# Weighted sums of an MoE layer: each set of gathers waits until the preceding pair's gathers of that set have landed

## What is computed

```python
shared_out = (silu(x @ Wsg.T) * (x @ Wsu.T)) @ Wsd.T      # 704 hidden columns
topk_scores, topk_idx = top_k(softmax(x @ Wr.T), 2)       # 8 experts, 2 for each token
out_e      = (silu(x @ Wg[e].T) * (x @ Wu[e].T)) @ Wd[e].T
routed_out = w1 * out_e[first expert] + w2 * out_e[second expert]
x = x + gb * (routed_out + shared_out)
```

## Time and profile before

| | before |
|---|---|
| median of 3 runs | 1712.21 us |
| the profiled execution, its own time | 1702.0 us |
| its span in the trace | 1700.3 us |
| PE busy in the span | 1643.6 us (97%) |
| late units with the weighted sums | 1540 to 1652 us of the span |
| late units behind them | 1652 to 1696 us |
| POOL's 64 gathers, first and last start | 1540.1, 1637.5 us |

### The profile page before, as it was taken

How to read it: one execution, slowest core, us unless ns; L and a number is a source line. 1 busy time by engine, 2 the same in 40 slices (tenths; PEclk the granted TensorE clock), 3 DMA queues, 4 the chain that set the end, 5 groups by cost and what they waited for, 6 DMA issues and landing times.

```text
span 1700.3 us, 26873 instructions
## 1 busy us (share of the span) xinstructions
PE 1643.6 (97%) x8817; PEld 1426.7 (84%) x8817; DVE 1326.2 (78%) x2553; ACT 770.3 (45%) x1138; POOL 417.9 (25%) x505
## 2 busy tenths in 40 slices
PE   4899999999989999999999999999999999999998
PEld 1578788888768888888888888999999999998997
DVE  3999999998698788888788775777777777776872
ACT  2444434333445555454545423555555555552331
POOL 2254444343322111323232351000000000006740
PEclk9999999999999999999999999999999999999999
DMA  9622222322544443655554689788878888866861
GB/s 317 222 76 93 80 99 74 99 74 75 202 149 154 151 149 123 223 183 201 180 197 173 223 318 312 240 287 298 286 259 279 284 299 285 266 219 215 277 209 38
DMA packets 138980, 335.32 MB, mean 197 GB/s; under 512 B 20568, under 2 KB 20568, under 8 KB 133232
## 3 DMA queue, kind: packets, MB, share of 16 engines
q1 hardware_dynamic: 103904, 248.09, 43.6%
q10 hardware_dynamic: 24720, 52.21, 8.6%
q0 software_dynamic: 10240, 33.56, 5.7%
HBM read 230.21 MB, written 103.60 MB: 196 GB/s over the span
## 4 chain that ended last, share of the span: by engine, by line
PE 73%; DVE 15%; DMA 4%; issue 3%; SPq 2%; ACT 2%; POOL 1%; DVEq 0%; ACTq 0%; POOLq 0%
PE bank L701 17%; PE bank L703 17%; PE bank L702 17%; PE bank L712 5%; PE bank L2412 5%; PE bank L2410 5%; PE bank L2411 5%; PE bank L2405 2%; DVE stage L1714 2%; DVE mix L1793 1%; DVE xm_lo L1799 1%; DMA expert_in_rows<-y_rows 1%; SPq L798 1%; DMA mod_rows<-ca_rows 1%; PE bank L2394 1%
## 5 line engine op out<-in xcount | busy, mean ns | idle before, releaser
L701 PE MATMUL bank<-gu_hi,ex_x_hl 128*128 128x352 f32 x1080 | 359.9, 333 | 0.1
L703 PE MATMUL bank<-gu_hi,ex_x_hl 128*128 128x352 f32 x1080 | 348.5, 323 | 0.0
L702 PE MATMUL bank<-gu_lo,ex_x_hl 128*128 128x352 f32 x1080 | 348.4, 323 | 0.0
L1281 POOL DMA_INDIRECT raw<-expert_out_rows,out_slots x64 | 74.9, 1170 | 536.7 <-DMA expert_out_rows<-y_rows 513.0
L701 PEld LDWEIGHTS bank<-gu_hi,ex_x_hl 128*128 128x128 f32 x1080 | 203.7, 189 | 0.4 <-issue 0.3
L702 PEld LDWEIGHTS bank<-gu_lo,ex_x_hl 128*128 128x128 f32 x1080 | 204.0, 189 | 0.0
L703 PEld LDWEIGHTS bank<-gu_hi,ex_x_hl 128*128 128x128 f32 x1080 | 203.3, 188 | 0.0
L1888 DVE TENSOR_TENSOR hid<-bank,sg_t 128x352 f32<-128x352 f32 x135 | 70.2, 520 | 126.8 <-PE bank L703 107.7
L2410 PE MATMUL bank<-dn_hi,hid_hi 128*128 128x512 f32 x405 | 161.7, 399 | 3.9 <-DVE hid_lo L1892 3.9
L2412 PE MATMUL bank<-dn_hi,hid_lo 128*128 128x512 f32 x405 | 160.0, 395 | 0.0
L2411 PE MATMUL bank<-dn_lo,hid_hi 128*128 128x512 f32 x405 | 158.7, 392 | 0.0
(11 more groups left out here) (257 smaller groups left out, 3835.9 us busy)
## 6 DMA issues: line engine op xcount, KB each, us to landing
raw<-in_ex_gu SPq DMA_DIRECT2D x40, 1408.0 KB, 6.5
raw<-in_ex_dn SPq DMA_DIRECT2D x40, 512.0 KB, 4.7
ex_x<-expert_in_rows SPq DMA_DIRECT2D x71, 256.0 KB, 6.3
expert_out_rows<-y_rows ACTq DMA_DIRECT2D x71, 256.0 KB, 6.1
h_rows<-h_t SPq DMA_DIRECT2D x64, 256.0 KB, 2.6
h_turned<-h_hl ACTq DMA_DIRECT2D x32, 512.0 KB, 3.0
ex_x_hl<-h_turned ACTq DMA_DIRECT2D x32, 512.0 KB, 3.7
x_t<-in_x SPq DMA_DIRECT2D x32, 256.0 KB, 2.7
```

The costliest lines, as they stand in the source:

```text
L701: pe.matmul(acc, act_hi[i], w_hi[i], start=(i == 0), stop=False)
L702: pe.matmul(acc, act_hi[i], w_lo[i], start=False, stop=False)
L703: last = pe.matmul(acc, act_lo[i], w_hi[i], start=False, stop=(i == chunks - 1))
L1281: pool.indirect_dma_start(rows[:, pair % 2, a, :], None, ys_d, bass.IndirectOffsetOnAxis(ap=out_slots[:, k, n:n + 1], axis=0)).then_inc(ar ...
```

## The change

Two lines are added on POOL. From pair 1 on, ahead of the two gathers of a set, POOL also waits until both gathers of the same set of the preceding pair have landed (32 more on that slot's semaphore). It is done set by set: y1 of a pair waits for y1 of the pair before, y2 for y2. Nothing else is edited; lines behind it move down by two, so the gathers' line L1281 becomes L1283.

```diff
                     if pair >= 2:
                         pool.wait_ge(*(cb_vec.done(pair - 2, "both") if k else cb_act.done(pair - 2, "first")))
+                    if pair:
+                        pool.wait_ge((y2_in if k else y1_in)[(pair - 1) % 2], 32 * ((pair - 1) // 2) + 32)
                     for a in range(2):
                         n = 2 * pair + a
```

## The result

The changed kernel took 1725.41 us (median of 10 runs) against 1717.02 us for the kernel before in the same comparison (10 runs). The ratio is 1.0048, with a 95% interval of 1.0034 to 1.0061: about 8 us slower. One of the ten executions after the change took 2040.21 us and is left out of the ratio; the median holds with or without it to 0.5 us. The range of the prediction ended at 1721.5 us. In its own terms, as a difference, +8.2 us stands against a forecast of +3.2 us, and lies between it and the rival in which the chain becomes the bound (+11.3 us).

A forecast was written before the change was run, and what follows sets the result against it. PE, busy 97% of the span, was taken as the bound; +2.5 us for the chain of waits and +0.7 us for the ramp on the 1712.2 us median gave 1715.4 us, range 1709.5 to 1721.5 us.

The forecast's parts named there:

- the chain becomes the bound: Rival for the gather stage: long landings stay in every second pair and PE waits; +11.3 us, 1723.5 us, chance 0.12.
- Bound and path: PE, busy 97%, bounds; loss comes through late gathers, `weighted` on DVE, then `hid_of`; at most 4.3 us to gain.
- Cost of a met wait: On POOL, a new wait that has already been met costs nothing visible.
- The link: POOL's y1 gathers: step, 4.9 us landing and 0.3 us; 13.37 us per two pairs, 0.89 us too long.
- The expectation that gathers held back leave the burst: Last stage: gathers held back 2 us miss the store and load burst, so the 6.7 us landing isn't carried over.
- The sum behind the link: Pairs 4 to 15: six cycles of 0.89 us, 5.3 us, less 2.8 us of slack, +2.5 us.
- Slack: Gathers land ahead of use: y1 by 2.8 us before ACT, y2 by 2.1 us before `weighted`; delay within it is free.
- The ramp: Pairs 1 to 3: only pair 3's y2 gathers start later, costing 0 to 1.5 us; +0.7 us taken.
- The signs I named: Profile after: landings at most about 4.9 us, more `weighted` waits in even pairs, PE idle about 7.5 us, unchanged before 1540 us.
- Nothing happens: Rival: held-back gathers land in 4.3 us or less, or waits are nearly always met; 1712.2 us, chance 0.20.
- The 2.6 us to land: Gather landing by the skill page's rule: link 4.2 us against 6.24 us, no gather late, no cost; 1712.2 us.
- The queue is relieved: Rival: at most four gathers under way land sooner, PE's idle times go; -2.4 us at most, 1709.8 us, chance 0.18.

The follow-up runs named there:

- e1: The changed kernel with each wait moved to the landing of the pair two before, so always met; 1.0007 of the kernel before.
- e2: The changed kernel with the new waits kept for the y1 sets alone; 1.0055 of the kernel before.
- e9: The changed kernel, waits kept, with three slots for each set instead of two; 1.0057 of the kernel before.
- e8: The changed kernel with the new waits kept for pairs 1 to 3 only; 0.9993 of the kernel before.
- e4: The changed kernel with each set waiting for the set issued just before it, at most two gathers under way; 1.0501 of the kernel before.
- e14: The kernel before, no new waits, two slots, each pair's products made two late units later; 0.9957 of the kernel before.
- e15: The kernel before, no new waits, two slots, products two late units later, run again on one chip with three variants; 0.9970 of the kernel before.
- e3: The changed kernel with the new waits kept for the y2 sets alone; 1.0035 of the kernel before.

## Why the prediction was wrong

*Bound and path.* Right. PE bounds the stage, the loss came through `weighted` on DVE, the rest of the program was not touched, and no gain came.

*Cost of a met wait.* Right: e1, 1.0007.

*The link.* Here is the step that failed, in two of its three terms. The first is "A set may now start only 0.3 us (the issue step) behind the landing". I read 0.3 us between two gathers that POOL issues in a row and used it for a gather that had to wait; e2 shows 0.70 to 0.84 us. The second is the time to landing: 4.9 us was the median of all gathers, where the second of each set counts, which took 5.35 us on average in the links of e2. My links were (13.37 / 2 =) 6.69 us per pair, those of e2 7.45 us: 0.45 us more from the step behind the landing, 0.45 us more from the landing, 0.14 us less from the step between the gathers. The change thus made gathers lag 2.4 us per two pairs in e2 and 1.9 us in the profile after (14.4 against 12.48 us), where I had 0.89 us. The expectation that gathers held back leave the burst was half right: in e2 the median fell from 4.9 to 4.2 us, the worst stayed (7.9 us).

*The sum behind the link.* With the corrected step alone, the working gives (1.25 + 4.9 + 0.75) + (1.72 + 4.9 + 0.75) = 14.27 us for two pairs and 6 x 1.79 - 2.8 = 7.9 us. That this meets the measured 8.2 us is luck: it leaves the second gather's landing at 4.9 us and the clock at nothing. With all of e2's link it gives 6 x (14.89 - 12.48) - 2.8 = 11.7 us, where PE's idle time in e2 is 9.5 us above that of e1. Multiplying by six cycles therefore overstates somewhat; by which of its parts, no run shows.

*Slack.* I took off 2.8 us, the slack of y1, and treated y2's chain apart. In e2 the loss arrives through y2, held back behind y1 on POOL, so y2's 2.1 us was the slack to take. e9 shows besides that slack can't be had from slots alone.

*The ramp.* Mis-sized: 0.7 us put, nothing measured (e8).

*The clock* was missing from the sum. In the profile after it accounts for about 3 of the 12.2 us.

*The signs I named.* The median landing at or under 4.9 us (in e2; the profile after has none) and the more frequent waits of `weighted` came true, though the longest fell in odd pairs (5 and 9), not in even ones. POOL waited more often than said (13 times), PE's idle time rose to 13.5 us instead of 7.5 us, and a difference did arise before 1540 us, with the chip.

*Rivals.* "Nothing happens" is refuted by the loss itself. The 2.6 us to land that I estimated from the Trainium skill (DMA: Bandwidth & Descriptors, section "Anatomy of one DMA — SWDGE (gpsimd) path") do not agree with the traces: the gathers of before, e2 and e4 took 3.3 to 7.9 us. "The queue is relieved" saw a real effect, shorter median landings, which is worth less than the waits cost. "The chain becomes the bound" is what happened, at its threshold rather than at its full price; I gave it 0.12. The range ended 4 us short of the measurement, and that part is not the mechanism: it was set around a median of three runs, 1712.2 us, where ten runs gave 1717.0 us. As a difference it went up to +9.3 us, and +8.2 us lies inside.

## What to carry to other kernels

A wait that lets a transfer start only when the one before it has landed turns a queue into a chain of round trips. Work out the link with the landing of the last transfer of a set, under the load of that stage, and with the step from a landing to the next start of an engine that had been waiting; compare it with the consumer's pace, and ask what a small error costs over all the links. Look also at what stands behind the waiting instruction on its engine: it starts late too, and may land last. More buffers gave such a chain nothing (e9) as long as it had no head start. The fastest version (e14, e15) had a use two units later and no throttling.

## What the runs showed of the hardware

- From a landing to the next start of POOL's indirect DMA: 0.70 to 0.84 us in e2 and 0.69 to 0.78 us in pairs 4 to 13 of e4, where POOL had to wait for the landing; 0.30 us between the end of one and the start of the next in a row. DVE and ACT started 0.05 to 0.12 us behind the landing they waited for (pair 13 of e2).
- The granted clock fell after a single idle time of PE of 3.17 us (to 0.60 on average in the next 6.24 us), but not after 2.21 us at 1629.9 us in the same execution; in e2 it fell to 0.73, 0.75 and 0.73 in the windows of 6.24 us with idle times of 1.95, 2.00 and 3.04 us and not with one of 2.22 us; and in before it stayed at 1.00 with one of 1.95 us. So the length of one idle time didn't decide it. In the profile after the price (3.2 to 3.4 us) was as large as the idle time itself.
- Fewer gathers under way landed sooner: median of the 64 gathers 4.9 us before, 4.4 us with the waits for y2 (e3), 4.2 us with those for y1 (e2), 3.5 us with two at most (e4).
- Chips differed by 1% on this kernel: 1700 us on one, 1716 to 1718 us on the others. In the profiles about 13 of these 16 us arise ahead of the first gather, in one stretch of 60 us around 1030 us.
